# Softmax probabilities of a graph-attention kernel: scaled once by VectorE, then split in whole-tile operations

## The chip, the cores and the metric

The kernel runs on one core of one Trainium2 chip. The metric is the device time of one execution in microseconds (us). Three runs of the kernel before gave 412.51, 413.01 and 413.43 us; the median is 413.01 us.

## What is computed

64 graphs of 128 nodes with 512 features each pass through one graph-attention layer with a residual. Everything is float32 at the interface.

```
h      = relu(layernorm(x))                       # 64 x 128 x 512
output = h @ weight                               # 512 x 512
q, k   = h @ wq, h @ wk
alpha  = max(q @ k^T, 0) * (adj != 0)             # 64 x 128 x 128
alpha  = softmax(alpha, axis=1)
out    = x + alpha @ output
```

## The kernel before, in words

**Precision.** Every matrix product is made of three float16 matmuls. Each float32 operand is split in a high part (a float16 copy, made by ScalarE) and a low part (the operand minus its high part, made by VectorE or GpSimd), and high x high, high x low and low x high are summed in PSUM. wq and wk are folded in one matrix m = wq wk^T at the start, so that a group needs t = h m, the scores t h^T, and v = h weight.

**Groups and periods.** The 64 graphs are worked in 16 groups of four graphs (GB = 4, G = 16). Groups 0 and 1 are written out plainly (`whole_product_t`, `whole_product_v`). From group 2 on, t and v are each made from seven half-size products instead of eight (a Strassen scheme: the names P1 to P7), and one call of `period` per engine does a group: group 2 written out, groups 3 to 10 in a loop unrolled four times, groups 11 to 14 written out, and group 15 (LAST) written out with an order of its own. The four tiles of a group's probabilities lie in one tensor of 128 partitions x (4 x 128).

**What a period does.** In the period of group g, TensorE makes eight of the fourteen products of group g, then the outputs of group g - 1 (`outs`, three matmuls for each of four graphs: `product_out`), then the other six products, and at the end the scores of group g. VectorE and ScalarE meanwhile turn the scores of group g - 1 into probabilities, prepare group g + 2 (layer norm, high parts) and split t and v of group g. GpSimd makes the scales of the layer norm and the low parts and Strassen sums of h for group g + 2. SyncE's queue does the transposes, loads and stores. Each engine works through a list in a fixed order, written by hand; semaphores tie the lists together.

**The softmax, and the lines of it that matter here.** All on group g - 1, in the period of group g:
- `softmax_shift` on VectorE: masked scores to `alpha` (L896), row maximum (L899), shift (L901).
- `exponentials` on ScalarE (L639): four operations, one a graph, to `exps`, with the row sums.
- `softmax_sum` on VectorE: row sums times 1/P_SCALE (L907), reciprocal to `row_inv` (L912), a 128 x 4 tile.
- `hi_of_p` on ScalarE (L663): for each of the four graphs `p_hi = exps * row_inv` as float16; the scale is a per-partition operand, one column of `row_inv` for each graph.
- `lo_of_p` on VectorE (L918): for each of the four graphs `p_lo = exps * row_inv - p_hi`, float16.
- `product_out` on TensorE (L1199 to L1201) uses `p_hi` and `p_lo`; `outs` waits for `p_split` before each graph and, before its fourth graph, for `out_read` of its first graph (the same PSUM bank is used again).
- `residual` on VectorE (L923) reads the outputs, adds x, and raises `out_read`.

**The order of VectorE in a period**: `softmax_shift`; layer norm statistics of two graphs (L841); `softmax_sum`; statistics of the two other graphs; the mask of the next group (L888); mean and variance x4 (L844); `lo_of_p` x4; low part of the first quadrant of t (L855); `sum_x_t` (L867); `sum_x_v` (L877, which waits for the last product ahead of `outs`); `residual` x4; sums and low parts of the rest. In the period of group 2 `residual` of the first graph stands ahead of `sum_x_t`.

**The order of ScalarE in a period**: `copy_p1_t` (L581), `exponentials`, `copy_p5_t`, `copy_p1_v`, `copy_p5_v` (L594), `hi_of_p` x4, the first high part of t (L600), then normalised h (L544) and its high parts (L554) for group g + 2, among them the first high part of v (L618), which waits for the outputs.

GpSimd's list begins a period with the scales of the layer norm (L411 to L418), which wait for mean and variance; then it makes low parts of h (L423), sums (L431 to L442) and low parts of the sums (L449).

In group 0, VectorE runs `softmax_shift`, one split of a weight tile (L995), `softmax_sum` and `lo_of_p` in a row; TensorE waits there for all four low parts (`p_split`) ahead of the outputs of group 0. In group 15 the low parts are GpSimd's (L516 multiplies `exps` by `row_inv` in one operation into a scratch tile, L523 subtracts).

Of the kernel before, what the change touches and what calls it, by code (L numbers as in the profile page):

```python
# [5 lines left out]
def graph_attention_kernel(nc, x, adj, weight, wq, wk, out):  # L6
# [13 lines left out]
    ALU = mybir.AluOpType  # L20
    ACT = mybir.ActivationFunctionType
    AX = mybir.AxisListType

    B, N, D = x.shape
    K = D // N
    GB = 4
    G = B // GB
    HG, HD, HK = GB // 2, D // 2, K // 2
    UNROLL = 4
    LAST = G - 1  # L30
# [16 lines left out]
    def later(g):  # L47

        return not (isinstance(g, int) and g == 0)
# [36 lines left out]
    with ctx:  # L86
        def sb(name, shape, dt):
            return ctx.enter_context(nc.sbuf_tensor(name, shape, dt))
# [4 lines left out]
        def sem(name):  # L93
            return ctx.enter_context(nc.semaphore(name))
# [67 lines left out]
        exps = sb("exps", [N, GB, N], F32)  # L162
        row_sum = sb("row_sum", [N, GB], F32)
        row_sum_s = sb("row_sum_s", [N, GB], F32)
        row_inv = sb("row_inv", [N, GB], F32)
        p_hi = sb("p_hi", [N, GB, N], F16)
        p_lo = sb("p_lo", [N, GB, N], F16)
# [71 lines left out]
        out_filled = sem("out_filled")  # L239
# [23 lines left out]
        exp_made = sem("exp_made")  # L263
        sum_scaled = sem("sum_scaled")
        inv_made = sem("inv_made")
        p_hi_made = sem("p_hi_made")
        p_split = sem("p_split")

# [263 lines left out]
        def _(act):  # L532
# [82 lines left out]
            def hi_of_v11(g):  # L615
                act.wait_ge(out_filled, GB * g)
                act.wait_ge(v_filled, made_v(g, N_P2))
                nc.scalar.activation(v_quadrant(0, 0), v_view(bank[VA][:]), ACT.Copy, scale=T_SCALE).then_inc(v_hi_made, 1)  # L618

            def hi_of_v22(g):  # L620
                act.wait_ge(v_summed, done(g, 2))
                nc.scalar.activation(v_quadrant(1, 1), v_view(c22_v), ACT.Copy, scale=T_SCALE).then_inc(v_hi_made, 1)

            def hi_of_v12(g):
                act.wait_ge(v_filled, made_v(g, N_P3))
                nc.scalar.activation(v_quadrant(0, 1), v_view(bank[VE][:]), ACT.Copy, scale=T_SCALE).then_inc(v_hi_made, 1)

            def hi_of_v21(g):
                act.wait_ge(v_filled, made_v(g, N_P4))
                nc.scalar.activation(v_quadrant(1, 0), v_view(bank[VB][:]), ACT.Copy, scale=T_SCALE).then_inc(v_hi_made, 1)  # L630
# [23 lines left out]
                nc.scalar.activation(tT_hi[:, c], t_bank(g)[c].rearrange("p (b n) -> p b n", b=GB), ACT.Copy,  # L654
                                     scale=T_SCALE).then_inc(t_hi, 1)

            def hi_of_p(g, graphs=range(GB)):

                act.wait_ge(inv_made, g + 1)
                if later(g):  # L660
                    act.wait_ge(out_filled, GB * g)
                for b in graphs:
                    nc.scalar.activation(p_hi[:, b], exps[:, b], ACT.Copy, scale=row_inv[:, b:b + 1]).then_inc(p_hi_made, 1)  # L663

# [105 lines left out]
            hi_of_h(2, 0, 3)  # L770
            exponentials(0)
            hi_of_p(0)
            hi_of_whole_t(1, 0)
            act.wait_ge(mt_summed, 4)
# [39 lines left out]
            hi_of_t21(LAST)  # L814
            exponentials(LAST)
            hi_of_v11(LAST)
            hi_of_p(LAST, range(HG + 1))
            hi_of_v12(LAST)
            hi_of_v22(LAST)
            hi_of_p(LAST, range(HG + 1, GB))  # L820
            hi_of_v21(LAST)

            act.wait_ge(s_split, sums(LAST, 4))
# [10 lines left out]
        def _(vec):  # L834
            def stats(g, s, loads, b):

                if b == 0:
                    vec.wait_ge(x_loaded[s], 16 * (loads - (s == 0)))
                    if later(g):
                        vec.wait_ge(rstd_made, g + 1)  # L840
                nc.vector.bn_stats(raw_stats[:, b], x_sb[:, s, b]).then_inc(stats_taken, 1)  # L841

            def mean_variance(g, b):
                nc.vector.bn_aggr(mean_var[:, b], raw_stats[:, b]).then_inc(meanvar_made, 1)  # L844
# [59 lines left out]
            def softmax_sum(g):  # L904

                vec.wait_ge(exp_made, GB * g + GB)
                nc.vector.tensor_scalar(row_sum_s[:], row_sum[:], 1.0 / P_SCALE, None,  # L907
                                        ALU.mult).then_inc(sum_scaled, 1)
                vec.wait_ge(sum_scaled, g + 1)
                if later(g):  # L910
                    vec.wait_ge(p_hi_made, GB * g)
                nc.vector.reciprocal(row_inv[:], row_sum_s[:]).then_inc(inv_made, 1)  # L912

            def lo_of_p(g):

                for b in range(GB):
                    vec.wait_ge(p_hi_made, GB * g + b + 1)
                    nc.vector.scalar_tensor_tensor(p_lo[:, b], exps[:, b], row_inv[:, b:b + 1], p_hi[:, b], ALU.mult,  # L918
                                                   ALU.subtract).then_inc(p_split, 1)

            def residual(g, s, b):
                vec.wait_ge(out_filled, GB * g + b + 1)
# [3 lines left out]
            def period(i, j, nxt=True, nxt2=True):  # L926

                g = i * UNROLL + j

                def stats2(b):  # L930
                    stats(g + 2, (j + 2) % UNROLL, i + (j + 2) // UNROLL + 1, b)

                softmax_shift(g - 1, (j + 1) % 2, i * (UNROLL // 2) + (j + 1) // 2)
                if nxt2:
                    stats2(0)
                    stats2(1)
                softmax_sum(g - 1)
                if nxt2:
                    stats2(2)
                    stats2(3)  # L940
                    vec.wait_ge(stats_taken, GB * (g + 2) + GB)
                if nxt:
                    make_mask(g + 1, (j + 1) % 2, i * (UNROLL // 2) + (j + 1) // 2 + 1)
                if nxt2:
                    for b in range(GB):
                        mean_variance(g + 2, b)
                lo_of_p(g - 1)
                lo_of_t(g, 0, bank[TA][:], 0, 0)
                if isinstance(g, int) and g == FIRST:

                    residual(g - 1, (j - 1) % UNROLL, 0)
                    sum_x_t(g)
                    sum_x_v(g)
                else:
                    sum_x_t(g)
                    sum_x_v(g)
                    residual(g - 1, (j - 1) % UNROLL, 0)
                for b in range(1, GB):
                    residual(g - 1, (j - 1) % UNROLL, b)
                sum_c22_t(g)  # L960
                lo_of_v(g, 0, bank[VA][:], 0, 0)
                sum_c22_v(g)
                lo_of_t(g, 1, c22_t, 1, 1)
                lo_of_t(g, 2, bank[TE][:], 0, 1)
                lo_of_t(g, 3, bank[TB][:], 1, 0)
                lo_of_v(g, 1, c22_v, 1, 1)
                lo_of_v(g, 2, bank[VE][:], 0, 1)
                lo_of_v(g, 3, bank[VB][:], 1, 0)
# [103 lines left out]
            softmax_shift(0, 0, 1)  # L1072
            lo_of_wt(2)
            softmax_sum(0)
            lo_of_p(0)
            lo_of_whole_t(1, 0)
            lo_of_whole_t(1, 1)
# [23 lines left out]
                period(g // UNROLL, g % UNROLL, nxt=g + 1 < G, nxt2=g + 2 < G)  # L1101
            softmax_shift(LAST - 1, (LAST - 1) % 2, (LAST - 1) // 2 + 1)
            softmax_sum(LAST - 1)
            lo_of_p(LAST - 1)
            sum_x_t(LAST)
            lo_of_t(LAST, 0, bank[TA][:], 0, 0)
# [347 lines left out]
```

## Time and profile before

| what | us |
|---|---|
| median of three runs | 413.01 |
| lowest and highest | 412.51, 413.43 |
| the profiled execution's own time | 412.91 |
| span of its profile | 411.1 |
| TensorE busy | 405.3 |
| VectorE busy | 298.1 |
| ScalarE busy | 277.7 |
| GpSimd busy | 264.7 |

The span is what the hardware profiler saw between the first and the last instruction; the execution's own time is 1.8 us longer. Busy times of different engines overlap, so they are compared with the span each by itself. PE stands for TensorE, PEld for its weight loads, DVE for VectorE, ACT for ScalarE, POOL for GpSimd, SP for SyncE. Matmuls are pipelined: a listed duration is longer than the distance to the next one.

### The profile page before, as it was taken

What the parts mean: (1) busy time and instruction counts of PE and PEld (TensorE: products, weight loads), DVE (VectorE), ACT (ScalarE), POOL (GpSimd) and SP (SyncE); (2) the same over time, 40 slices, a digit from 0 to 9 for tenths busy, and PEclk for the clock granted to TensorE, in tenths of its full rate; (3) what the DMA queues carried; (4) which work ended last, traced back from release to release, by engine and by line L of the source; (5) the groups of instructions that cost most, each with busy time, mean ns of one, the idle gap of its engine ahead of it and who ended that gap; (6) DMA issues with size and microseconds to landing.
All of it is one profiled execution on the core that took longest, in us unless ns stands there. A gap on an engine that the chain in (4) does not pass through costs nothing.

```text
span 411.1 us, 9529 instructions
## 1 busy us (share of the span) xinstructions
PE 405.3 (99%) x3580; PEld 321.7 (78%) x3580; DVE 298.1 (73%) x571; ACT 277.7 (68%) x592; POOL 264.7 (64%) x286
## 2 busy tenths in 40 slices
PE   8999999999999999999999999999999999999995
PEld 5444545979797997979798897979889797979884
DVE  5797789896867676776767777676777667656565
ACT  4749887765867677766777776776867777644534
POOL 0767896979495866759395775939577584910004
PEclk9999999999999999999999999999999999999999
DMA  8973858989889897997969498985978599493022
GB/s 284 373 110 67 217 103 217 232 205 217 181 208 191 245 155 212 189 204 188 192 212 196 156 214 199 197 218 173 198 241 158 156 220 181 75 197 112 2 104 102
DMA packets 161641, 75.03 MB, mean 183 GB/s; under 512 B 135360, under 2 KB 143808, under 8 KB 161600
## 3 DMA queue, kind: packets, MB, share of 16 engines
q1 hardware_dynamic: 161168, 73.81, 77.6%
q8 instruction: 28, 0.46, 0.5%
q10 hardware_dynamic: 432, 0.66, 0.4%
q14 instruction: 13, 0.11, 0.1%
HBM read 24.12 MB, written 16.78 MB: 99 GB/s over the span
## 4 chain that ended last, share of the span: by engine, by line
PE 90%; DVE 4%; DMA 2%; ACT 1%; SPq 1%; issue 1%; POOL 0%; DVEq 0%; POOLq 0%
PE bank L1166 10%; PE bank L1165 10%; PE bank L1163 10%; PE bank L1181 10%; PE bank L1180 10%; PE bank L1178 10%; PE s_bank L1192 3%; PE s_bank L1193 3%; PE s_bank L1194 3%; PE bank L1199 2%; PE bank L1200 2%; PE bank L1201 2%; PE bank L1320 2%; PE bank L1322 2%; PE bank L1321 2%; DMA x_sb<-in_x 2%
## 5 line engine op out<-in xcount | busy, mean ns | idle before, releaser
L423 POOL TENSOR_TENSOR hn_lo<-h,hn_hi 128x512 f16<-128x512 f32 x64 | 74.0, 1166 | 53.1 <-ACT hn_hi L554 52.9
L544 ACT ACTIVATE h<-x_sb,shift,rstd 128x512 f32<-128x512 f32 x64 | 50.0, 804 | 24.0 <-POOL shift L418 23.6
L449 POOL TENSOR_TENSOR hn_lo<-s,hn_hi 128x512 f16<-128x512 f32 x56 | 63.3, 1163 | 0.3 <-ACT hn_hi L559 0.3
L1163 PE MATMUL bank<-hT_hi,mt_hi 128*128 128x256 f16 x224 | 61.1, 273 | 0.0
L1165 PE MATMUL bank<-hT_lo,mt_hi 128*128 128x256 f16 x224 | 61.1, 273 | 0.0
L1180 PE MATMUL bank<-wt_lo,hT_hi 128*128 128x256 f16 x224 | 61.1, 273 | 0.0
L1166 PE MATMUL bank<-hT_hi,mt_lo 128*128 128x256 f16 x224 | 61.1, 273 | 0.0
L1178 PE MATMUL bank<-wt_hi,hT_hi 128*128 128x256 f16 x224 | 61.1, 273 | 0.0
L1181 PE MATMUL bank<-wt_hi,hT_lo 128*128 128x256 f16 x224 | 61.1, 273 | 0.0
L559 ACT ACTIVATE hn_hi<-s 128x512 f16<-128x512 f32 x56 | 33.8, 625 | 25.6 <-POOL s L438 19.9
L1180 PE MATMUL bank<-w_lo,hT_hi 128*128 128x256 f16 x168 | 45.8, 273 | 0.0
L1166 PE MATMUL bank<-hT_hi,m_lo 128*128 128x256 f16 x168 | 45.8, 273 | 0.0
L1181 PE MATMUL bank<-w_hi,hT_lo 128*128 128x256 f16 x168 | 45.8, 273 | 0.0
L1165 PE MATMUL bank<-hT_lo,m_hi 128*128 128x256 f16 x168 | 45.8, 273 | 0.0
L1178 PE MATMUL bank<-w_hi,hT_hi 128*128 128x256 f16 x168 | 45.8, 273 | 0.0
L1163 PE MATMUL bank<-hT_hi,m_hi 128*128 128x256 f16 x168 | 45.8, 273 | 0.0
L855 DVE SCALAR_TENSOR_TENSOR tT_lo<-bank,tT_hi 128x512 f16<-128x512 f32 x42 | 28.9, 688 | 22.5 <-ACT tT_hi L612 17.5
L1193 PE MATMUL s_bank<-tT_lo,hT_hi 128*128 128x128 f16 x256 | 43.7, 219 | 0.0
L1194 PE MATMUL s_bank<-tT_hi,hT_lo 128*128 128x128 f16 x256 | 43.7, 219 | 0.0
L1192 PE MATMUL s_bank<-tT_hi,hT_hi 128*128 128x128 f16 x256 | 43.7, 219 | 0.0
L860 DVE SCALAR_TENSOR_TENSOR v_lo<-bank,v_hi 128x512 f16<-128x512 f32 x40 | 27.3, 683 | 21.1 <-ACT v_hi L630 21.1
L639 ACT ACTIVATE exps<-alpha,shift_max,s_unscale 128x128 f32<-128x128 f32 x64 | 30.8, 482 | 13.1 <-DVE shift_max L901 13.1
(169 smaller groups left out, 1115.2 us busy)
## 6 DMA issues: line engine op xcount, KB each, us to landing
out_h<-x_sb SPq DMA_DIRECT2D x63, 256.0 KB, 2.1
x_sb<-in_x SPq DMA_DIRECT2D x15, 1024.0 KB, 5.5
adj_sb<-in_adj SPq DMA_DIRECT2D x16, 256.0 KB, 5.3
hn_hi<-in_L_gnn_wq SPq DMA_DIRECT2D x4, 256.0 KB, 5.6
x_sb<-in_x SPq DMA_DIRECT2D x2, 512.0 KB, 7.2
w_sb<-in_L_gnn_weight SPq DMA_DIRECT2D x2, 512.0 KB, 8.7
hn_lo<-in_L_gnn_wk ACTq DMA_DIRECT2D x2, 256.0 KB, 3.8
hn_lo<-in_L_gnn_wk SPq DMA_DIRECT2D x2, 256.0 KB, 3.7
```

Of the source, the lines that this page charges most:

```text
L423: nc.gpsimd.tensor_tensor(hn_lo[:, s, b], h[:, b], hn_hi[:, s, b], ALU.subtract).then_inc(h_split, 1)
L449: nc.gpsimd.tensor_tensor(low, s32[:, f], high, ALU.subtract).then_inc(s_split, 1)
L544: nc.scalar.activation(h[:, b], x_sb[:, s, b], ACT.Relu, bias=shift[:, b:b + 1], scale=rstd[:, b:b + 1]).then_inc(h_made, 1)
L1163: nc.tensor.matmul(o, bh[:, k, cols], ah[:, :, k], start=first and c == 0 and k == 0, stop=False, skip_group_check=True)
L1165: nc.tensor.matmul(o, bh[:, k, cols], al[:, :, k], start=False, stop=False, skip_group_check=True)
L1166: last = nc.tensor.matmul(o, bl[:, k, cols], ah[:, :, k], start=False, stop=k == HK - 1, skip_group_check=True)
L1178: nc.tensor.matmul(o, ah[:, r, k], bh[:, k], start=first and r == 0 and k == 0, stop=False, skip_group_check=True)
L1180: nc.tensor.matmul(o, ah[:, r, k], bl[:, k], start=False, stop=False, skip_group_check=True)
L1181: last = nc.tensor.matmul(o, al[:, r, k], bh[:, k], start=False, stop=k == HK - 1, skip_group_check=True)
L1192: nc.tensor.matmul(o, hT_hi[:, s, b, k], tT_hi[:, k, b], start=k == 0, stop=False)
L1193: nc.tensor.matmul(o, hT_hi[:, s, b, k], tT_lo[:, k, b], start=False, stop=False)
L1194: last = nc.tensor.matmul(o, hT_lo[:, s, b, k], tT_hi[:, k, b], start=False, stop=k == K - 1)
```

## The change

For groups 0 to 14 VectorE multiplies the exponentials of all four graphs by their reciprocal row sums in one `tensor_tensor`, in place, right after the reciprocal (`probabilities`, with a new semaphore `p_made`; `row_inv` is broadcast along the 128 columns). The high part is then one ScalarE copy of the whole 128 x 512 tile without a scale, and waits for `p_made`; the low part is one VectorE subtraction of the whole tile. Semaphore counts are kept by adding 4 at once. Group 15 keeps its order: its high parts are still made graph by graph from `exps` and `row_inv` (`hi_of_last_p`), its low parts by GpSimd. The reciprocal of a group waits for the multiplication of the group before in place of its high parts.

```diff
-            def hi_of_p(g, graphs=range(GB)):
-
-                act.wait_ge(inv_made, g + 1)
+            def hi_of_p(g):
+
+                act.wait_ge(p_made, g + 1)
                 if later(g):
                     act.wait_ge(out_filled, GB * g)
+                nc.scalar.activation(p_hi[:], exps[:], ACT.Copy).then_inc(p_hi_made, GB)
+
+            def hi_of_last_p(g, graphs):
+
+                act.wait_ge(inv_made, g + 1)
+                act.wait_ge(out_filled, GB * g)
                 for b in graphs:
                     nc.scalar.activation(p_hi[:, b], exps[:, b], ACT.Copy, scale=row_inv[:, b:b + 1]).then_inc(p_hi_made, 1)
...
-            hi_of_p(LAST, range(HG + 1))
+            hi_of_last_p(LAST, range(HG + 1))
...
-            hi_of_p(LAST, range(HG + 1, GB))
+            hi_of_last_p(LAST, range(HG + 1, GB))
...
                 if later(g):
-                    vec.wait_ge(p_hi_made, GB * g)
+                    vec.wait_ge(p_made, g)
                 nc.vector.reciprocal(row_inv[:], row_sum_s[:]).then_inc(inv_made, 1)
 
+            def probabilities(g):
+
+                vec.wait_ge(inv_made, g + 1)
+                nc.vector.tensor_tensor(exps[:], exps[:], row_inv[:].unsqueeze(2).to_broadcast([N, GB, N]),
+                                        ALU.mult).then_inc(p_made, 1)
+
             def lo_of_p(g):
 
-                for b in range(GB):
-                    vec.wait_ge(p_hi_made, GB * g + b + 1)
-                    nc.vector.scalar_tensor_tensor(p_lo[:, b], exps[:, b], row_inv[:, b:b + 1], p_hi[:, b], ALU.mult,
-                                                   ALU.subtract).then_inc(p_split, 1)
+                vec.wait_ge(p_hi_made, GB * g + GB)
+                nc.vector.tensor_tensor(p_lo[:], exps[:], p_hi[:], ALU.subtract).then_inc(p_split, GB)
...
                 softmax_sum(g - 1)
+                probabilities(g - 1)
...
             softmax_sum(0)
+            probabilities(0)
             lo_of_p(0)
...
             softmax_sum(LAST - 1)
+            probabilities(LAST - 1)
             lo_of_p(LAST - 1)
```

## Rows read from the trace of the kernel before

**Rows 1.** The page, its first two parts: busy time by engine, TensorE's granted clock
```profile
PE 405.3 (99%) x3580; PEld 321.7 (78%) x3580; DVE 298.1 (73%) x571; ACT 277.7 (68%) x592; POOL 264.7 (64%) x286
...
PEclk9999999999999999999999999999999999999999
```

**Rows 2.** Busy time by window: window, length, then busy us (x instructions) by engine
```profile
31.80:57.70 25.90, 25.90 (x156) 13.09 (x156) 19.52 (x30) 23.24 (x48) 22.11 (x21) 1.00 0.65 145
57.70:85.00 27.30, 27.27 (x210) 18.43 (x210) 24.98 (x47) 18.04 (x39) 23.34 (x25) 1.00 0.84 197
85.00:404.00 319.00, 319.00 (x3093) 274.09 (x3091) 224.92 (x444) 216.94 (x473) 201.68 (x205) 1.00 0.79 179
```

**Rows 3.** Who waited for whom: total us, times, longest
```profile
DVE bank L877 <- PE bank L1181: 16.2, 11, 1.7
...
PEld bank L1199 <- DVE p_lo L918: 0.5, 1, 0.5
```

**Rows 4.** Timeline at group 0's probabilities: start, us, engine, line, operation
```profile
57.52 0.38 PE L1322 MATMUL bank<-hT_hi,m_lo 128*128 128x512 f16 x1
57.93 0.39 PE L1199 MATMUL bank<-v_hi,p_hi 128*128 128x512 f16 x1
...
53.09 1.28 ACT L663 ACTIVATE p_hi<-exps,row_inv 128x128 f16<-128x128 f32 x4 [0.66 <-DVE row_inv L912]
...
53.53 4.34 DVE L918 SCALAR_TENSOR_TENSOR p_lo<-exps,row_inv,p_hi 128x128 f16<-128x128 f32 x4 [0.47 <-ACT p_hi L663]
...
52.78 2.31 POOL L423 TENSOR_TENSOR hn_lo<-h,hn_hi 128x512 f16<-128x512 f32 x2
```

**Rows 5.** Groups of instructions by form, VectorE and ScalarE: busy us, mean ns | idle before
```profile
L867 DVE TENSOR_TENSOR bank<-bank,spare 128x512 f32<-128x512 f32 x14 | 9.6, 689 | 0.2 <-PE bank L1166 0.2
...
L559 ACT ACTIVATE hn_hi<-s 128x512 f16<-128x512 f32 x56 | 33.8, 625 | 25.6 <-POOL s L438 19.9 <-POOL s L442 2.8 <-POOL s L434 2.1
L663 ACT ACTIVATE p_hi<-exps,row_inv 128x128 f16<-128x128 f32 x64 | 20.4, 390 | 0.7 <-DVE row_inv L912 0.7
```

**Rows 6.** Timeline in the period of group 9, where the pattern is settled
```profile
243.56 0.18 DVE L912 RECIPROCAL row_inv<-row_sum_s 128x4 f32<-128x4 f32 x1
...
245.75 1.11 DVE L918 SCALAR_TENSOR_TENSOR p_lo<-exps,row_inv,p_hi 128x128 f16<-128x128 f32 x4
246.77 0.68 DVE L855 SCALAR_TENSOR_TENSOR tT_lo<-bank,tT_hi 128x512 f16<-128x512 f32 x1
...
249.52 0.70 DVE L877 TENSOR_TENSOR bank<-bank,spare 128x512 f32<-128x512 f32 x1 [1.46 <-PE bank L1181]
250.17 0.75 DVE L923 SCALAR_TENSOR_TENSOR x_sb<-bank,out_unscale,x_sb 128x512 f32<-128x512 f32 x1
...
244.77 1.26 ACT L663 ACTIVATE p_hi<-exps,row_inv 128x128 f16<-128x128 f32 x4
...
252.11 0.60 ACT L618 ACTIVATE v_hi<-bank 128x512 f16<-128x512 f32 x1 [1.19 <-PE bank L1201]
...
238.98 4.50 POOL L449 TENSOR_TENSOR hn_lo<-s,hn_hi 128x512 f16<-128x512 f32 x4
...
251.26 0.38 PE L1199 MATMUL bank<-v_hi,p_hi 128*128 128x512 f16 x1
```

**Rows 7.** Timeline in the period of group 3: first residual, fourth output
```profile
108.65 0.74 DVE L923 SCALAR_TENSOR_TENSOR x_sb<-bank,out_unscale,x_sb 128x512 f32<-128x512 f32 x1
...
109.60 0.38 PE L1199 MATMUL bank<-v_hi,p_hi 128*128 128x512 f16 x1
```

**Rows 8.** Timeline in the period of group 2: GpSimd busy beside the probabilities
```profile
81.70 2.64 DVE L918 SCALAR_TENSOR_TENSOR p_lo<-exps,row_inv,p_hi 128x128 f16<-128x128 f32 x4
...
84.90 0.75 DVE L923 SCALAR_TENSOR_TENSOR x_sb<-bank,out_unscale,x_sb 128x512 f32<-128x512 f32 x1
...
78.93 4.74 POOL L449 TENSOR_TENSOR hn_lo<-s,hn_hi 128x512 f16<-128x512 f32 x4
...
85.99 0.38 PE L1199 MATMUL bank<-v_hi,p_hi 128*128 128x512 f16 x1
```

More of the change, by code:

```diff
@@ L265, in graph_attention_kernel @@
         inv_made = sem("inv_made")
+        p_made = sem("p_made")
         p_hi_made = sem("p_hi_made")
```

## The prediction, made before the changed kernel ran

> **What bounds the kernel now.** I read the page first: TensorE is busy 405.3 of 411.1 us, no other engine over 298.1, and the granted clock is full in every slice [rows 1]. A share of 99% can still hide small stops, so next come busy times by window. From 31.8 to 57.7 us TensorE has no idle time at all; from 57.7 to 85.0 it lacks 0.03 us, and the 319.0 us from 85 to 404 are all busy [rows 2]. Matmuls overlap, though, so a busy window may hide a stop shorter than an operation's tail. For that I read the starts: matmuls of 512 columns follow each other every 0.21 to 0.22 us, and at one place there is more, from 57.52 to 57.93 [rows 4], 0.41 us where 0.21 are usual: a stop of 0.20 us. The waits name what it was, the low parts of group 0's probabilities [rows 3]. It is the one place where TensorE waits for what this change touches, outside group 15, which keeps its code. So the ceiling of any gain is 0.20 us, and all else that VectorE and ScalarE save or spend is free as long as TensorE never has to wait for it. The question is how near it comes to waiting.
>
> **The change, part by part.** *What it removes and adds on VectorE*, for each of 15 groups: four operations of 128 x 128 go, which in the settled period take 1.02 us of the list (from 245.75 to 246.77) [rows 6]. One subtraction of 128 x 512 comes, and one multiplication of the same size. Neither form is in the trace on these operands; the nearest row is a `tensor_tensor` on 128 x 512 float32, 689 ns [rows 5], of which about 0.09 us overlap with the next operation (the four low parts are listed with 1.11 us and their follower starts after 1.02) [rows 6], so 0.60 us of the list each. Net: 0.60 + 0.60 - 1.02 = 0.18 us more in a period. *On ScalarE*: four operations of 1.26 us together [rows 6] become one copy without a scale operand; the same form on the same size is L559, 625 ns [rows 5]. ScalarE gains 0.64 us a period, or 9.6 us over 15 groups, all of it beside TensorE and so worth nothing by itself.
>
> *The new wait.* The high part now waits for the multiplication. In the settled period the reciprocal starts at 243.56 and the multiplication can run from about 243.65 to 244.34, while ScalarE reaches the high part only at 244.77 [rows 6]: the copies ahead of it cover the wait by 0.4 us. If that cover were gone, the first high part of t and the layer norm of group g + 2 would be late by as much, and ScalarE's own saving of 0.64 us would pay for it.
>
> *What is queued behind the multiplication on VectorE.* First the two statistics, the mask, mean and variance: 0.60 us later each. GpSimd waits for these with its scales, and ScalarE for the scales with h. That chain runs into an idle 1.19 us of ScalarE ahead of L618, which waits for TensorE's outputs [rows 6]; 0.60 us fit in, and nothing after L618 moves. In the first periods, where that idle is smaller, the first high part of v comes up to 0.60 us late; behind it VectorE has the sum that TensorE asks for five products later, and with fourteen products, scores and outputs in a period of 23.6 us ((251.26 - 109.60) / 6, groups 3 to 9) [rows 6, 7] five products are over 6 us. No term. SyncE's queue waits for GpSimd's parts of h a period ahead; also no term.
>
> *The tight place.* The fourth output of a group needs the bank of the first, which `residual` frees. In the settled period the residual ends at 250.92 and the matmul starts at 251.26, 0.34 us later; but VectorE stood idle for 1.46 us before L877, so 0.18 us more work ahead of it changes nothing [rows 6]. 11 of the 14 periods show such an idle stretch, 16.2 us in all [rows 3]. In the period of group 3 there is none, VectorE goes back to back up to the residual, which ends at 109.39 against a matmul at 109.60: 0.21 us [rows 7]. Taking off 0.06 us for the signal (in group 0 the last low part ended at 57.87 and the matmul followed at 57.93 [rows 4]), 0.15 are left against 0.18 of added work: TensorE loses 0.03 us there, once.
>
> *Where GpSimd is busy beside it.* Two places show VectorE slowed. In group 0 the four low parts took 4.34 us and in group 2's period 2.64 us [rows 4, 8], against 1.11 us in the settled one [rows 6]; what differs is that GpSimd works through both of the slow stretches, with operations of about 1.15 us, and pauses between 243.48 (238.98 + 4.50) and the scales in the settled one. So one operation of VectorE with two SBUF inputs waits there for an operation of GpSimd: a mean of 1.09 us for 128 columns where 0.28 (1.11 / 4) is normal, some 0.8 us a time. The Trainium skill has the rule, in "SBUF — State Buffer", the section on the engine and DMA sides: the pair of ports that VectorE and GpSimd share is an exclusive lock held for a whole instruction, taken by VectorE operations with two SBUF inputs. It speaks for fewer operations, but also against adding one; the trace agrees with it where GpSimd is busy. A large operation here would cost between 0.60 us (no collision) and 0.60 + 1.16, about 1.8 us (a whole GpSimd operation, 2.31 / 2 [rows 4]).
>
> For group 0: the high part could start at 53.09, the reciprocal done [rows 4]; so the multiplication runs from there to between 53.8 and 54.9, the copy with its signal takes 0.7 us more, and the subtraction ends between 55.2 and 57.4. All of it lies ahead of 57.73, when TensorE comes to the outputs: the stop of 0.20 us goes. Range of this term: 0.00 to -0.20, and I take -0.20. What is late next is nothing before 60 us.
>
> For the period of group 2: the list ahead of the residual gains 2.56 to 2.64 us by the four low parts that go and gets back two operations of 0.60 to 1.8 us each: between -1.4 and +1.0 us. The residual ends at 85.65 against a matmul at 85.99; less the signal 0.28 us are left [rows 8]. So the term lies between 0 and +0.7 us. In the middle of that span, at -0.2, the list gets shorter, and the term is 0.
>
> *The sum*: -0.20 + 0.03 + 0 = -0.17 us against the profiled execution, 412.91 us, hence 412.74. That execution stands 0.10 us under the median of the runs shown, so the forecast is 412.8 us, which is no change: a measurement of this kernel can tell about 0.2%, 0.8 us, from none.
>
> **The rivals.** *A, two collisions in every period: slower.* It would sit between the reciprocal and `sum_x_v` in the settled periods. For it: GpSimd's last low part ends at 243.48, only 0.17 us ahead of the multiplication, and the scales of the layer norm, now later, come beside the subtraction. One collision costs up to 1.16 us, two up to 2.3. It decides once the added work exceeds the idle 1.46 us plus the 0.28 us of the residual, 1.74 in all; 0.18 + 2.3 = 2.5 us is over that by 0.75, and in 11 periods this makes 8 us: 421 us. Against it: GpSimd's list would have to move later by more than its pause lets it, and one collision alone stays inside (1.34 of 1.74). The lock that the Trainium skill describes in "SBUF — State Buffer" would be the mechanism: both new operations have two SBUF inputs. Chance 0.03.
>
> *B, the start-up periods collide badly: within the noise, or just above.* Groups 2 and 3 lose 0.7 us and some 0.2 us and group 0 gains nothing: 413.01 + 0.9 = 413.9 us. For it: GpSimd is busy without a pause beside both operations of group 2 [rows 8]. Against it: the four that go are paying four waits there now. Chance 0.08; half of it over the 0.8 us.
>
> *C, the broadcast operand or the in-place write makes the multiplication slow,* say twice 0.69 us. The change would then not do what it says, VectorE would have 0.9 us more a period, still under 1.74; group 3 alone would lose 0.75 us: 413.6 us. For it: no row shows the form on VectorE. Against it: no row shows such a penalty either, and the operand is small and read again and again. Chance 0.04.
>
> *D, a gain beyond the stop.* TensorE has no other idle time that probabilities cause, so only a disturbed comparison could show it. Chance 0.03.
>
> **How the numbers follow.** The forecast has 0.82. Its own range is the spread of the runs shown, 412.51 to 413.43, less 0.2 at the lower end: 412.3 to 413.4. Taking in B and C and a little of the scatter of medians gives 412.2 to 413.9; A stays outside. Within 0.2%: the forecast, half of B and most of C, 0.90. Slower: A, half of B, and a little, 0.06. Faster: 0.04.
>
> **What the profile of the changed kernel would show.** Right: no stop of TensorE at 57.7 us, TensorE busy 405 us as before, 15 multiplications of about 0.69 us, ScalarE down by 9 to 10 us of busy time, VectorE's idle stretch ahead of L877's counterpart down from 1.46 to about 1.3 us, and ScalarE's idle ahead of the first high part of v down from 1.19 to about 0.6 us. Wrong: a first matmul of a fourth output that follows its predecessor by more than 0.22 us in the settled periods (A), or in those of groups 2 and 3 (B, C); a multiplication whose shortest instance is well over 0.7 us (C).

## The result, and the profile after

| | before | after |
|---|---|---|
| median of nine runs, us | 413.00 (412.51 to 413.43) | 413.94 (413.42 to 414.82) |
| profiled execution, us | 412.91 | 413.79 |

The ratio is 1.0024, with a 95% interval of 1.0014 to 1.0035: slower by 0.9 us, against a forecast of 412.8 us and no change, with 413.9 us as the upper end of its range.

The page of the kernel after, its first line of busy times and the line of the chain that ended last:

```profile
PE 405.3 (98%) x3580; PEld 321.9 (78%) x3580; DVE 301.2 (73%) x541; ACT 268.3 (65%) x547; POOL 267.9 (65%) x286
...
PE 77%; ACT 6%; DVE 6%; POOL 4%; issue 3%; DMA 2%; SPq 1%; DVEq 0%; ACTq 0%; POOLq 0%
```

TensorE does the same 405.3 us of work as in [rows 1]. ScalarE is down by 9.4 us, as forecast, VectorE is up by 3.1 us, and GpSimd, whose code is the same, by 3.2 us: the first hint, since GpSimd can only have been held up. TensorE's share of the chain is 77%, where the page of the kernel before has 90%. The work of three other engines has come onto the path.

Busy times by window, for the stretches of [rows 2] (window, length, then busy us of PE, PEld, DVE, ACT, POOL):

```profile
31.60:57.50 25.90, 25.90 (x156) 13.20 (x157) 18.09 (x29) 21.76 (x44) 22.08 (x21) 1.00 0.63 141
57.50:85.00 27.50, 26.69 (x207) 18.08 (x206) 25.18 (x42) 18.26 (x38) 23.40 (x25) 1.00 0.88 196
85.00:404.00 319.00, 318.88 (x3087) 273.58 (x3085) 229.07 (x417) 208.11 (x433) 204.06 (x203) 1.00 0.79 179
```

TensorE lacks 0.81 us in the second window, where it lacked 0.03, and 0.12 in the third. The exact places show in the starts of matmuls. The timeline of TensorE after:

```profile
57.34 0.38 PE L1336 MATMUL bank<-hT_hi,m_lo 128*128 128x512 f16 x1
57.55 0.38 PE L1213 MATMUL bank<-v_hi,p_hi 128*128 128x512 f16 x1
...
83.55 0.27 PE L1195 MATMUL bank<-wt_hi,hT_lo 128*128 128x256 f16 x1
84.64 0.39 PE L1213 MATMUL bank<-v_hi,p_hi 128*128 128x512 f16 x1 [0.81 <-DVE p_lo L930]
...
109.98 0.38 PE L1215 MATMUL bank<-v_hi,p_lo 128*128 128x512 f16 x1
110.48 0.38 PE L1213 MATMUL bank<-v_hi,p_hi 128*128 128x512 f16 x1
```

At 57.5 us the matmuls follow each other in 0.21 us: the stop of 0.20 us in [rows 4] is gone, as forecast. Two others are new. In the period of group 2 the first output waits for the low part: 1.09 us from start to start where 0.11 is usual after 256 columns, a stop of 0.98 us. In the period of group 3 the fourth output comes 0.50 us after its predecessor in place of 0.21: 0.29 us. No other is added. -0.20 + 0.98 + 0.29 = +1.07 us; this execution also came 0.18 us sooner to the matmuls at 31 us (31.55 against 31.73, a difference of the start), which leaves the 0.88 us between the two profiled executions.

VectorE after, in the period of group 2 (answers to [rows 8]), in that of group 3 (to [rows 7]) and in the settled period of group 9 (to [rows 6]):

```profile
79.00 0.18 DVE L919 RECIPROCAL row_inv<-row_sum_s 128x4 f32<-128x4 f32 x1
79.21 1.39 DVE L924 TENSOR_TENSOR exps<-exps,row_inv 128x512 f32<-128x512 f32 x1
...
81.83 1.19 DVE L895 TENSOR_SCALAR mask<-adj_sb 128x512 bf16<-128x512 int32 x1
...
83.23 1.35 DVE L930 TENSOR_TENSOR p_lo<-exps,p_hi 128x512 f16<-128x512 f32 x1
84.50 0.68 DVE L862 SCALAR_TENSOR_TENSOR tT_lo<-bank,tT_hi 128x512 f16<-128x512 f32 x1
...
104.29 0.18 DVE L919 RECIPROCAL row_inv<-row_sum_s 128x4 f32<-128x4 f32 x1
...
109.60 0.74 DVE L934 SCALAR_TENSOR_TENSOR x_sb<-bank,out_unscale,x_sb 128x512 f32<-128x512 f32 x1
...
244.46 0.18 DVE L919 RECIPROCAL row_inv<-row_sum_s 128x4 f32<-128x4 f32 x1
244.67 0.69 DVE L924 TENSOR_TENSOR exps<-exps,row_inv 128x512 f32<-128x512 f32 x1
...
247.39 0.66 DVE L930 TENSOR_TENSOR p_lo<-exps,p_hi 128x512 f16<-128x512 f32 x1
...
250.40 0.70 DVE L884 TENSOR_TENSOR bank<-bank,spare 128x512 f32<-128x512 f32 x1 [1.14 <-PE bank L1195]
```

The multiplication takes 0.69 us where nothing disturbs it and 1.39 beside GpSimd, the subtraction 0.66 and 1.35. The whole low part is there at 84.58 us, the matmul starts at 84.64. In the kernel before, the four low parts of [rows 8] came one by one. Windows on the same trace that hold one of them each show the first two:

```profile
81.70 0.95 DVE L918 SCALAR_TENSOR_TENSOR p_lo<-exps,row_inv,p_hi 128x128 f16<-128x128 f32 x1
...
82.58 1.24 DVE L918 SCALAR_TENSOR_TENSOR p_lo<-exps,row_inv,p_hi 128x128 f16<-128x128 f32 x1
```

The first graph's low part was there at 82.65 us, 1.93 us before the whole tile of the kernel after.

GpSimd after, around the same low part:

```profile
78.89 5.13 POOL L450 TENSOR_TENSOR hn_lo<-s,hn_hi 128x512 f16<-128x512 f32 x4
83.99 0.64 POOL L412 TENSOR_TENSOR var_eps<-mean_var,eps 128x4 f32<-128x4 f32 x1
...
86.24 0.20 POOL L419 TENSOR_TENSOR shift<-neg_mean,rstd 128x4 f32<-128x4 f32 x1
...
247.55 0.56 POOL L412 TENSOR_TENSOR var_eps<-mean_var,eps 128x4 f32<-128x4 f32 x1 [3.18 <-DVE mean_var L851]
...
249.71 0.20 POOL L419 TENSOR_TENSOR shift<-neg_mean,rstd 128x4 f32<-128x4 f32 x1
```

The first two of these took 4.74 us [rows 8] and 0.24 us in the kernel before. GpSimd's addition of four columns now lasts 0.64 us and ends 0.05 us after VectorE's subtraction: it waited for it. So the two hold each other up, and not only in the first periods: even the settled period has 0.56 us there, where the kernel before has 0.21.

### The profile page after: what moved, and what is told of

Read it like the earlier page. It is cut to its first block, busy times and chain, and to the rows that moved or that the text cites. A ratio compares the mean times of both kernels' runs of the same rounds, so it can differ in the third digit from the quotient of the medians.

```text
span 412.0 us, 9470 instructions
## 1 busy us (share of the span) xinstructions
PE 405.3 (98%) x3580; PEld 321.9 (78%) x3580; DVE 301.2 (73%) x541; ACT 268.3 (65%) x547; POOL 267.9 (65%) x286
## 4 chain that ended last, share of the span: by engine, by line
PE 77%; ACT 6%; DVE 6%; POOL 4%; issue 3%; DMA 2%; SPq 1%; DVEq 0%; ACTq 0%; POOLq 0%
PE bank L1177 10%; PE bank L1179 10%; PE bank L1180 10%; PE bank L1194 10%; PE bank L1195 10%; PE bank L1192 10%; PE s_bank L1208 3%; PE s_bank L1207 3%; PE s_bank L1206 3%; PE bank L1213 2%; PE bank L1214 2%; PE bank L1215 2%; ACT h L545 2%; DMA x_sb<-in_x 2%; ACT hn_hi L555 1%
## 5 line engine op out<-in xcount | busy, mean ns | idle before, releaser
L862 DVE SCALAR_TENSOR_TENSOR tT_lo<-bank,tT_hi 128x512 f16<-128x512 f32 x42 | 28.8, 687 | 22.3 <-ACT tT_hi L613 18.3
```

## Where the time is made: experiments

The kernel before ran again beside each of these kernels, with medians of 412.60 to 412.76 us. So times are best compared by the ratio (the change itself: 1.0024), and single stops by the starts of matmuls.

**The stop in group 2's period.** The first run takes the change back for group 1 alone.

```diff
+    def by_graph(g):
+        return isinstance(g, int) and g == 1
...
             def hi_of_p(g):
+                if by_graph(g):
+                    hi_of_last_p(g, range(GB))
+                    return
...
             def probabilities(g):
+                if by_graph(g):
+                    return
...
             def lo_of_p(g):
+                if by_graph(g):
+                    for b in range(GB):
+                        vec.wait_ge(p_hi_made, GB * g + b + 1)
+                        nc.vector.scalar_tensor_tensor(p_lo[:, b], exps[:, b], row_inv[:, b:b + 1], p_hi[:, b], ALU.mult,
+                                                       ALU.subtract).then_inc(p_split, 1)
+                    return
```

> The changed kernel, with the probabilities of group 1 alone (worked in the period of group 2) in the old form: no multiplication, four scaled high parts, four scaled low parts. Theory (the stop of TensorE of 0.98 us at the first output in that period is made there, by the whole-tile low part coming late): that stop goes, the one of 0.29 us in the period of group 3 stays, the time is 0.9 to 1.0 us under the changed kernel, 413.0 us. Rival (the stop is an echo of group 0's new form, which starts GpSimd's low parts of the sums 0.7 us later): the stop stays within 0.2 us of 0.98, and the time at 413.9 us. Second rival (the stop of 0.29 us in the period of group 3 is inherited from the longer one before it): it goes too, 412.8 us.

Measured: 413.35 us, ratio to the kernel before 1.0018 (1.0007 to 1.0028), expected 413.0. The 0.98 us went; 0.12 us came at the third output of that period, and the stop in group 3's period did not stay at 0.29 us but grew to 0.60. The cause of the first stop is shown; neither rival's number came. (Gone and come back: -0.98 + 0.12 + 0.31 us, which is why the time is over the 413.0 us expected.) That TensorE was 0.86 us sooner at group 3's period and gave 0.31 of it back there says that something else sets the time at that point. TensorE there, with the wait named:

```profile
109.08 0.38 PE L1235 MATMUL bank<-v_hi,p_lo 128*128 128x512 f16 x1
109.89 0.38 PE L1233 MATMUL bank<-v_hi,p_hi 128*128 128x512 f16 x1 [0.43 <-DVE x_sb L954]
```

**Group 0 alone in the new form** asks the same of the forecast's one gain. The edit is that of the run before but for the condition:

```diff
+    def by_graph(g):
+        return later(g)
```

> The kernel before, with group 0's probabilities alone in the new form. The forecast's term for group 0 by itself. First reading (the term is worth its 0.20 us): no stop at 57.7 us and none later, 0.2 us under the kernel before. Second reading (the periods of groups 2 and 3 are set by VectorE, ScalarE and GpSimd, and TensorE, being earlier, waits there instead): no stop at 57.7 us, but 0.1 us at an output in the period of group 2, as in the run with group 1 in the old form, and 0.1 to 0.3 us at the fourth output in that of group 3, and a time within 0.15 us of the kernel before.

Measured: 412.84 against 412.71 us, ratio 1.0002 (0.9993 to 1.0011). The second reading holds: no stop at 57.7 us, but 0.11 us at the third output of group 2's period, 0.05 at a matmul of its scores (at 95.6 us) and 0.12 at the fourth output of group 3's, 0.28 in all for the 0.20 won. The gain is worth nothing.

**Is it GpSimd that stretches VectorE?**

```diff
             sums_of_h(3, 1)
+            pool.wait_ge(p_split, 2 * GB)
             lows_of_sums(3, 1)
```

> The changed kernel, with GpSimd held back once: its four low parts of the sums of group 3 wait for the low parts of group 1's probabilities. Theory (GpSimd's operations are what stretches VectorE's): in the period of group 2 the multiplication takes 0.69 us in place of 1.39, the mask 0.43 in place of 1.19, the low part 0.66 in place of 1.35; together 2.1 us less, and the first output does not wait at all. GpSimd's list is then some 5 us later in that period and the next, so a stop may come up in later periods; that is no term of the theory. Rival (VectorE is stretched by DMA traffic of the start-up or by something else than GpSimd): durations stay over 1.1 us and the stop over 0.7 us.

VectorE of that kernel, with GpSimd held back from 78.7 to 82.3 us:

```profile
78.98 0.69 DVE L925 TENSOR_TENSOR exps<-exps,row_inv 128x512 f32<-128x512 f32 x1
...
80.90 0.43 DVE L896 TENSOR_SCALAR mask<-adj_sb 128x512 bf16<-128x512 int32 x1
...
81.53 0.66 DVE L931 TENSOR_TENSOR p_lo<-exps,p_hi 128x512 f16<-128x512 f32 x1
```

All three numbers are as expected, and the stop is gone; the rival on DMA falls. GpSimd itself was then late, and three stops at 92 to 99 us (0.79, 1.58 and 0.97 us) and one of 0.42 us at the fourth output of group 3's period brought the time to 416.1 us in its one run: the remedy costs more than the illness.

**Collision or grain?** Grain is the size of what is handed over at once. This kernel makes the low parts one graph at a time, on the multiplied tile:

```diff
-                nc.vector.tensor_tensor(p_lo[:], exps[:], p_hi[:], ALU.subtract).then_inc(p_split, GB)
+                for b in range(GB):
+                    nc.vector.tensor_tensor(p_lo[:, b], exps[:, b], p_hi[:, b], ALU.subtract).then_inc(p_split, 1)
```

> The changed kernel, with the low parts subtracted graph by graph (four operations on 128x128 from the multiplied tile), the multiplication and the one high part kept. Theory (late start and collisions first, grain second): in the period of group 2 the first low part starts at about 83.2 us as the whole one did and takes until 83.6 to 84.2, so the first output waits 0.1 to 0.6 us in place of 0.98, and later ones may wait for the later low parts; in all other periods VectorE's list gets 0.4 us longer, so the stop at the fourth output in the period of group 3 grows from 0.29 to about 0.7 us. Time 413.6 to 414.2 us. Rival (grain alone: all four low parts arriving together is the whole cause): the stop of group 2's period is under 0.1 us.

Measured: 414.3 us, ratio 1.0042 (1.0025 to 1.0059). The stop of group 2's period was 0.22 us, inside the range given, that of group 3's 0.65; but in group 0, where TensorE waits for all four low parts and GpSimd is busy, there was a stop of 0.72 us, which the expectation did not have. Small operations release the first output earlier, and any of them can meet GpSimd: one of the four did in group 2's period (0.94 us against 0.28 for the others), two in group 0's (1.36 and 1.35 us). The finer grain takes 0.76 of the 0.98 us away and the absence of GpSimd all of it, so both are in the 0.98 us, and neither alone makes it.

**The subtraction earlier, in group 2's period only**, ahead of the mask and of mean and variance:

```diff
+                    if isinstance(g, int) and g == FIRST:
+                        lo_of_p(g - 1)
                     vec.wait_ge(stats_taken, GB * (g + 2) + GB)
...
-                lo_of_p(g - 1)
+                if not (isinstance(g, int) and g == FIRST):
+                    lo_of_p(g - 1)
```

> The changed kernel; in the period of group 2 alone the whole-tile subtraction comes right after the statistics, ahead of the mask and of mean and variance, 1.4 us earlier in the list. Theory: it starts at about 81.8 us, takes up to 1.35 us beside GpSimd, and is done at 83.2 us, ahead of TensorE at 83.66: the stop of 0.98 us goes. Mean and variance come 1.3 us later, at 84.2 us; GpSimd is free at 84.0 us, so its scales start 0.3 to 0.6 us later, and with them h, the high parts and the period of group 3, where the stop may grow from 0.29 to 0.9 us. Time 413.0 to 413.6 us. If the stop of 0.98 us stays, the place in the list is not what makes it.

Measured: 414.54 us, ratio 1.0037 (1.0025 to 1.0049): a miss. The first output did not wait any more, but the third did, by 0.61 us. It writes the bank from which the first low part of t is read; VectorE and TensorE of that kernel:

```profile
85.05 0.65 DVE L862 SCALAR_TENSOR_TENSOR tT_lo<-bank,tT_hi 128x512 f16<-128x512 f32 x1
...
85.03 0.38 PE L1218 MATMUL s_bank<-v_hi,p_lo 128*128 128x512 f16 x1
85.85 0.38 PE L1216 MATMUL bank<-v_hi,p_hi 128*128 128x512 f16 x1 [0.44 <-DVE tT_lo L862]
```

The low part ends at 85.70 us, the matmul starts 0.15 later. This is also the 0.12 us of the run with group 1 in the old form. Mean and variance were late, GpSimd with them, and the scores at 96 us waited 0.71 us; at the fourth output of group 3's period the stop grew from 0.29 to 0.43 us. The subtraction itself took 1.56 us.

**The stop in group 3's period.**

```diff
                     sum_x_t(g)
-                    sum_x_v(g)
                     residual(g - 1, (j - 1) % UNROLL, 0)
+                    sum_x_v(g)
```

> The changed kernel, with the first residual ahead of sum_x_v in every period from group 3 on, so that VectorE has 0.6 us less ahead of it. Theory (the 0.29 us at the fourth output of group 3's period are VectorE's list, 0.30 us longer by the change, against 0.21 us of room): that stop goes, the one of 0.98 us stays, 413.6 us; sum_x_v has over 3 us of room and costs nothing. Rival (the stop has another cause, such as the stop before it): it stays at 0.2 to 0.3 us, 413.9 us.

Measured: 413.60 us, ratio 1.0017 (1.0008 to 1.0027). The stop of 0.98 us is as it was (1.00), that of 0.29 is gone, and the time is as expected. The starts of the matmuls show it; the two ratios, 1.0017 and 1.0024, are too near each other to do so. With the early subtraction as well:

> The changed kernel with both moves: the early subtraction in the period of group 2, and the first residual ahead of sum_x_v from group 3 on. Theory: neither stop is left, TensorE runs without a gap from 31.5 to 404 us, and the time is 412.5 to 412.8 us, at or 0.2 us under the kernel before. Rival (being later by mean and variance, group 3's period shows its stop at another wait): 413.0 to 413.4 us.

413.88 us, ratio 1.0024 (1.0015 to 1.0033): 0.63 us at the third output and 0.70 at the scores were there, both still in group 2's period. The theory failed, and the rival, which had a stop in group 3's period and at most 413.4 us, did not come either. With group 1 in the old form instead:

> The changed kernel, with group 1 in the old form and the first residual ahead of sum_x_v from group 3 on. If the two stops are independent and each has the cause given: 0.1 us left at the third output of group 2's period, none in that of group 3, 1.1 us under the changed kernel, 412.6 us against about 412.8 for the kernel before. If the time of group 3's period is held by something other than VectorE's list, a stop of up to 0.6 us stays at one of its outputs and the time is 413.2 us.

412.67 against 412.71 us, ratio 0.9995 (0.9985 to 1.0004): one stop of 0.12 us and one of 0.05 are left, and the loss is undone. It is the best version found, and no faster than the kernel before by this measurement.

**What holds group 3's period: a loop.** VectorE's mean and variance let GpSimd make its scales; ScalarE makes h with them, GpSimd the sums, ScalarE in its fixed order the last high part of v, VectorE the last low part and then the shift of the softmax, and so the next reciprocal. One way round, a turn, takes a period. Its two posts in the kernel before, on VectorE and GpSimd, for groups 2 and 3 and for the settled period:

```profile
103.64 0.18 DVE L912 RECIPROCAL row_inv<-row_sum_s 128x4 f32<-128x4 f32 x1
...
85.58 0.20 POOL L418 TENSOR_TENSOR shift<-neg_mean,rstd 128x4 f32<-128x4 f32 x1
...
247.84 0.20 POOL L418 TENSOR_TENSOR shift<-neg_mean,rstd 128x4 f32<-128x4 f32 x1
```

From the start of GpSimd's last scale (`shift`) to the next reciprocal it is 85.58 to 103.64, 18.06 us, in the kernel before, and 86.24 to 104.29, 18.05, after; in nine turns of the kernel with three extra multiplications below, in which TensorE waits and cannot be what holds the loop up, it is 18.01 to 18.17. From the reciprocal to `shift` it is 4.28 us before in the settled period (243.56 to 247.84) and 5.25 after (244.46 to 249.71). A turn takes at least 22.3 us before and 23.3 after, against TensorE's period of 23.6. TensorE sets the pace, but of 1.3 us of room a turn, 0.3 are left. In the period of group 2 there is no room at all: GpSimd is still at its low parts when mean and variance are there, the reciprocals of groups 1 and 2 are 24.61 us apart before and 25.29 after, both over 23.6, and so the other engines, not TensorE, fix when VectorE's list of group 3's period begins. Three runs load this loop. One useless multiplication in the periods of groups 3 to 10:

```diff
             def probabilities(g):
+                if not isinstance(g, int):
+                    for _ in range(1):
+                        nc.vector.tensor_tensor(alpha[:], exps[:], exps[:], ALU.mult)
                 vec.wait_ge(inv_made, g + 1)
```

> The changed kernel with one more 128x512 multiplication on VectorE, of the exponentials by themselves into a tile that nothing reads, ahead of the real one in the periods of groups 3 to 10. It adds 0.6 us to the list of each. Theory (from group 4's period on VectorE has 1.1 us of idle ahead of sum_x_v and more, so that only group 3's period pays): the stop at the fourth output of group 3's period grows from 0.29 to 0.9 us, the idle ahead of sum_x_v falls from 1.14 to 0.5 us, TensorE has no stop in the periods of groups 5 to 10, and the time is 0.6 us over the changed kernel, 414.5 us. Rival (work on VectorE costs TensorE time in every period, as a sum over periods): 8 x 0.6 = 5 us more, 418.7 us.

Measured: 415.05 us in three runs, expected 414.5. The reciprocals stand 23.7 us apart and TensorE stops by 0.11 to 0.26 us in five of the seven periods after group 3's: neither the theory as it stood (no stop) nor the rival (0.6 us in each). The loop, worked out from this run, explains it: 5.70 us from the reciprocal to `shift` and 18.02 back are 23.72 us. Three of them, two more into scratch tiles:

> The same with three such multiplications in each of the periods of groups 3 to 10, 1.8 us added to each list. Theory (the room in the settled periods is the 1.14 us of idle plus 0.2 us between residual and fourth output, 1.34 in all): group 3's period loses 1.8 us more, each of the seven periods after it is 0.5 us over its room and shows a stop of about that at an output, and the time is 413.9 + 1.8 + 3.4 = 419 us. If the room is larger than that (because what is late once stays late and is not paid again, VectorE being ahead again once TensorE has waited), the settled periods show stops in the first one or two periods only, and the time is 415.7 to 416.7 us.

Measured: 425.3 us in two runs (the ratio is 1.031, 1.027 to 1.035) for an expected 419. Timeline of VectorE, GpSimd and ScalarE, one turn, with the wait at each step of the loop:

```profile
255.30 0.18 DVE L921 RECIPROCAL row_inv<-row_sum_s 128x4 f32<-128x4 f32 x1
...
280.23 0.18 DVE L921 RECIPROCAL row_inv<-row_sum_s 128x4 f32<-128x4 f32 x1
...
260.05 0.55 POOL L414 TENSOR_TENSOR var_eps<-mean_var,eps 128x4 f32<-128x4 f32 x1 [4.83 <-DVE mean_var L853]
...
262.21 0.20 POOL L421 TENSOR_TENSOR shift<-neg_mean,rstd 128x4 f32<-128x4 f32 x1
...
262.54 1.52 ACT L547 ACTIVATE h<-x_sb,shift,rstd 128x512 f32<-128x512 f32 x2 [3.48 <-POOL shift L421]
...
274.37 0.63 ACT L562 ACTIVATE hn_hi<-s 128x512 f16<-128x512 f32 x1 [1.78 <-POOL s L441]
274.90 0.58 ACT L633 ACTIVATE v_hi<-bank 128x512 f16<-128x512 f32 x1
...
275.52 0.69 DVE L869 SCALAR_TENSOR_TENSOR v_lo<-bank,v_hi 128x512 f16<-128x512 f32 x1 [1.71 <-ACT v_hi L633]
276.13 0.68 DVE L905 SCALAR_TENSOR_TENSOR alpha<-s_bank,maskT 128x512 f32<-128x512 f32 x1
```

6.91 us to `shift` and 18.02 back: 24.93 us, and TensorE's fourth outputs of these two periods stand at 238.21 and 263.15, 24.94 apart. TensorE stops twice between them, 0.74 us at a first output and 0.60 at the fourth. The loop, and not TensorE, is the bound in these periods. The room of 1.34 us on which the expectation rested was never there to spend. Last, the one extra operation behind mean and variance:

```diff
                         mean_variance(g + 2, b)
+                if not isinstance(g - 1, int):
+                    nc.vector.tensor_tensor(alpha[:], exps[:], exps[:], ALU.mult)
                 lo_of_p(g - 1)
```

> The changed kernel with the same one extra multiplication as in the run before, in the same periods, but put behind mean and variance, ahead of the low part. Loop theory (from the reciprocal through mean and variance, GpSimd's scales, ScalarE's h, GpSimd's sums, ScalarE's last high part of v and VectorE's shift back to the next reciprocal runs a loop that takes 5.25 + 18.02 = 23.27 us in the changed kernel and 22.3 us in the one before, against TensorE's 23.6 us a period; one extra ahead of mean and variance made it 23.7 us and cost TensorE 0.1 us in every period): here the extra stands outside the loop, the time from the reciprocal to the shift of h stays within 0.1 us of 5.25, the stop at the fourth output of group 3's period grows to 0.9 us, and no period after it shows a stop; the time is 414.5 us. Rival (the room between VectorE's list and the residual is all that counts): small stops of 0.1 to 0.3 us in the periods of groups 4 to 10 as in the run before, 415.0 us or more.

Measured: 415.7 us, ratio 1.0072 (1.0056 to 1.0089). This is what the rival had forecast: after group 3's period the stops are those of the run with the operation ahead, within 0.05 us. Either the loop is refuted or the expectation was wrong in where it ends, and the time from the reciprocal to `shift` decides. GpSimd in that kernel:

```profile
107.51 0.55 POOL L412 TENSOR_TENSOR var_eps<-mean_var,eps 128x4 f32<-128x4 f32 x1 [3.32 <-DVE mean_var L851]
108.02 0.65 POOL L413 TENSOR_TENSOR neg_mean<-mean_var,minus_one 128x4 f32<-128x4 f32 x1
```

The second took 0.19 us in the changed kernel. The extra operation and the subtraction each hold up one of GpSimd's small ones; from the reciprocal to `shift` it is 5.71 us, where 5.25 had been expected, as much as with the operation ahead. So an operation with two SBUF inputs beside GpSimd's scales is in the loop even behind mean and variance. This was read after the result; no further run tested it.

## Why the prediction was wrong

- **What bounds the kernel, the removed stop, ScalarE's saving, 0.69 us for the multiplication, rival C**: right. TensorE is the bound, the stop of 0.20 us went, ScalarE saved 9.4 us for a forecast 9.6, and the broadcast operand costs nothing.
- **The step that failed is "the tight place"**, as applied to group 2's period. It asked only whether the fourth output would find its bank free, after `residual`. That did come out as bounded: the list from the reciprocal to L862 grew from 5.23 us (79.03 to 84.26) to 5.50, inside -1.4 to +1.0 us. But the first output waits for the low part, and the single subtraction makes the first graph's low part ready only with the last one's. The old form handed over its first of four after 0.95 of the 2.64 us. TensorE came at 83.66 us, the tile at 84.58. A bound of the ready time of what the first output reads would have shown it: the low parts started at 81.70 us in [rows 8]; 0.6 to 1.8 us for the multiplication ahead of them and as much for the subtraction give 82.9 to 85.3 us, on either side of the 83.85 at which TensorE would come (its first output had started at 84.05, less the 0.20).
- **The middle of a span was taken for its value.** Both operations collided, at 1.39 and 1.35 us. The list up to L862 did not get 0.2 us shorter but 0.27 longer. The row of the four slow low parts, from the same stretch, was there to say so, but it was read as four waits of some 0.8 us; taken singly, two of the four waited (0.95 and 1.24 us) and the two others took 0.34 us each. So the old form did not pay four waits, as the case against rival B had it, but two, and the new one pays two as well.
- **Group 3's period**: forecast 0.03 us, measured 0.29, a term mis-sized. The list grew by 0.30 us in place of 0.18 (from reciprocal to residual 5.31 us after and 5.01 before), because the multiplication starts 0.21 us after the reciprocal and the statistics had started 0.10 after it. And the signal cost 0.14 us there (residual ended at 110.34, matmul at 110.48), not 0.06. That makes 0.30 - (0.21 - 0.14) = 0.23 us; the rest is that the reciprocal came 0.65 us later than before (104.29 against 103.64) and TensorE only 0.59 (first output at 84.64 against 84.05).
- **"ScalarE is idle there, 0.60 us fit in", "no term"** for the layer norm: true of the period that was looked at, and not of the loop. The room was 1.3 us a turn and the change took 1.0 of it: 0.74 on VectorE up to mean and variance and 0.23 by holding up GpSimd behind them. ScalarE's idle ahead of the first high part of v, forecast at 0.6 us, was 0.20. The spent room is also why the kernel before is back at TensorE's pace of 23.6 us from reciprocal to reciprocal after two periods (22.5, 23.0, 23.6) and the one after only after six (23.4, 23.3, 23.3, 23.2, 23.5, 23.5, 23.6).
- **The gain of 0.20 us in group 0** was rightly found and yet worth nothing, and not for what the change does to the settled periods: with group 0 alone in the new form the loop has its old times (4.28 us, 18.05 us), and the 0.20 us came back as stops all the same. The reciprocals of groups 1 and 2 are 24.61 us apart in that run, as before; TensorE came sooner to periods whose timing the other engines set.
- **The rivals**: B had the right mechanism in part and nearly the right time, 413.9 us at the upper edge of the range, with a chance of 0.08. That its time is so near is luck: its price of 0.9 us came from the residual and not from the first output, and it had group 0 gain nothing. A's 1.74 us of room in the settled period is refuted: one extra operation of 0.6 us already stopped TensorE in settled periods.
- In "SBUF — State Buffer", the section on the two separate sides, the Trainium skill calls the port pair that VectorE and GpSimd share an exclusive lock, held for the whole instruction. The traces agree, in both directions: 0.69 to 1.39 us for VectorE, 0.24 to 0.64 us for four columns on GpSimd, and both gone in group 2's period of the run in which GpSimd waits (0.69 and 0.20 us). The forecast used only one direction.

## What to carry to other kernels

When small operations are merged in one, ask who reads the first piece and when, not only how long the list gets: the merged operation hands over everything at its end. Idle time in front of a wait is no free room if the same engine is part of a loop over the iterations; measure the loop with the bounding engine left out (here 18.05 + 4.28 us) and compare it with the period. A new VectorE operation with two SBUF inputs also has a price on GpSimd, and a stop removed early in such a pipeline may only move.

## What was not expected of the hardware

- Additions and multiplications of four columns on GpSimd went from 0.24 to 0.64 us, and from 0.19 to 0.65, beside VectorE operations with two SBUF inputs.
- Two SBUF inputs are not the only thing that makes a VectorE operation wait: the mask, made from one SBUF tile, took 1.07 us before and 1.19 after beside GpSimd and 0.43 with GpSimd held back. The two statistics in the same stretch took the same 0.66 to 0.69 us each with GpSimd at work and without.
- From the end of a VectorE operation to the matmul that waits for it took 0.06 us when it had written SBUF from SBUF (84.58 to 84.64) and 0.14 to 0.15 us when it had read PSUM (110.34 to 110.48; 85.70 to 85.85 in the run with the early subtraction). Which of the two differences of these operations makes it was not tried.
- The long arm of the loop, `shift` to reciprocal, took 18.01 to 18.17 us in nine turns of the kernel with three extra multiplications; so much regularity in a chain through three engines had not been expected. With group 1 in the old form it was up to 18.33 us, for a reason that was not looked for.
